# Chosen experts of a two-layer decoder: four places for the weighed rows, and weights laid out in pieces of 2 KB

## The chip, the cores and the metric

The kernel runs on one core of a Trainium2 chip. The metric is the device time of one execution in microseconds, the median of several runs. Before the change it is 2603.03 us (3 runs, 2599.43 to 2603.57).

## What is computed

The program is a two-layer decoder on 8 sequences of 512 tokens, width 256. Only its last part matters here, the mixture of experts of layer 1: 64 experts, each token goes to its 8 best, no more than 160 tokens an expert. Cut to that:

```python
def _swiglu(x, w1, w2):
    h = x @ w1.T
    x1, x2 = jnp.split(h, 2, axis=-1)
    return x1 * jax.nn.silu(x2) @ w2.T
# x: 4096 tokens x 256; expert_w1: 64 x 1536 x 256; expert_w2: 64 x 256 x 768
shared_out = _swiglu(x, shared_w1, shared_w2)
w_topk, idx_topk = jax.lax.top_k(softmax(x @ wg.T), 8)       # then w_topk / sum
buf = zeros((64, 160, 256)).at[expert, rank].set(x[token])   # gather by expert
h = jnp.einsum('ech,efh->ecf', buf, expert_w1)
x1, x2 = jnp.split(h, 2, axis=-1)
out = jnp.einsum('ecf,ehf->ech', x1 * jax.nn.silu(x2), expert_w2)
combined = zeros((4096, 256)).at[token].add(out * weight)
return shared_out + combined
```

## The kernel before

All arithmetic is float32. `mix_experts_sparse` is the last phase. Its first block computes the shared expert, the gates and, for each expert, the list of its tokens. It also writes normalised rows with their gates to `token_rows` in HBM, and the residual stream to `out_x` in HBM. SyncE loads the weights of experts 0 and 1 during this block.

Its second block is the part for the chosen experts; it takes the last 0.7 ms. Each engine walks over the 64 experts in the same order (`experts_in_turn`, L2077), four experts to a turn (`GATHERED`). An expert has 160 rows: 128 **main rows** (`xa`, `index_a`, `oa`) and 32 **tail rows**; the tails of four experts share one tile (`xb`, `index_b`, `ob`, 32 partitions, a "quad", for each).

- SyncE loads expert e's weights with two DMAs (`load_expert`, L2118 and L2119) as soon as expert e-2 has done its first products (the wait on `h_full` of `after_first_product`, L2515). `w1` has two places, `w2` four.
- TensorE, for each expert: 48 products of the first layer (L2616, six steps of eight, into three places of `hp`), then 12 of the second layer (L2623, into `op`), in whose middle it transposes the next expert's gathered rows (L2588, L2592). After an odd expert it does the second layer for the tails of the pair (`tails`, L2602).
- ScalarE applies silu (L2640). VectorE multiplies the halves (L2684) and so frees a place of `hp` (`h_free`); in between it weighs the main rows of the expert before (L2661: `op` times the gate, to `oa`, counted by `weighed`), and after each pair the tails (L2674, L2676, to `ob`).
- GpSimd adds the weighed rows to `out_x` by indirect DMAs with addition (`scatter`, L2529) and gathers the rows of expert e+4 (L2130, tails L2136). Two scatters may hit the same token, so a main scatter waits until all scatters of the experts before it have landed (semaphore `added`).

The places of `oa` are kept by the semaphore `rows_free`. GpSimd puts 2 in at the start (L2573), and one more each time an expert's turn comes in which all earlier main scatters have landed (L2549 for even places, L2553 for odd ones). VectorE waits at L2660 for `rows_free` to reach e+1 before it weighs expert e. Its queue is in order: while it waits there, the products of L2684 for the current expert wait behind it, no place of `hp` comes free, and TensorE's next step of L2616 waits. `tails_free` does the same for the single place of `ob` (L2554).

The weights lie in HBM as one array, a row for each expert and partition: 3072 numbers (12 KB) for `w1` and 1536 (6 KB) for `w2`. A DMA of L2118 so reads 128 pieces of 12 KB, one of L2119 128 pieces of 6 KB.

Of the kernel before, what the change touches and what calls it, by code (L numbers as in the profile page):

```python
# [16 lines left out]
P = 128  # L17
B, S, D = 8, 512, 256
NT = B * S // P
TB = S // P  # L20
DC = D // P
# [2048 lines left out]

GATHERED = 4


# [10 lines left out]
def mix_experts_sparse(nc, ctx, x, ident, stats, mean, rstd, w_gate, w_exp, sw_in, sw_out, rows, out):  # L2084


    with ExitStack() as own:
        k = Kit(nc, own, "me_")
# [27 lines left out]
        def load_expert(sp, e, place, w2_of):  # L2116
            one = w_exp[bass.ds(e, 1)].rearrange("a p n -> p (a n)")
            sp.dma_start(w1[:, place % 2].rearrange("p c n -> p (c n)"), one[:, 0:DC * 2 * F]).then_inc(w1_loaded[place % 2], 16)  # L2118
            sp.dma_start(w2_of.rearrange("p c n -> p (c n)"), one[:, DC * 2 * F:]).then_inc(w2_loaded[place], 16)  # L2119

# [372 lines left out]
        hid = k.sb("hid", [P, 2, FC, CAP])  # L2493
        oa = k.sb("oa", [P, 2, D])
        ob = k.sb("ob", [P, D])
# [15 lines left out]
        with nc.Block() as block:  # L2511
# [15 lines left out]
            def _(pool):  # L2527
# [8 lines left out]
                def turn(i, first, last):  # L2536
# [3 lines left out]
                    for m in range(GATHERED):  # L2540
# [5 lines left out]
                        if m % 2 == 0:  # L2546
                            all_added(i * (32 * GATHERED), 32 * m)
                            if not (first and m == 0):
                                pool.sem_inc(rows_free, 1)  # L2549
                            scatter(oa[:, m % 2, :], then_a[:, m % 2, :])  # L2550
                        else:
# [10 lines left out]
                            pool.sem_inc(passed, 1)  # L2562
                            scatter(oa[:, m % 2, :], then_a[:, m % 2, :])
                            scatter(ob[quad(m), :], then_b[:, 1, :])
# [7 lines left out]

                pool.sem_inc(rows_free, 2)  # L2573
                pool.sem_inc(tails_free, 1)
# [70 lines left out]
            def _(dve):  # L2645
# [11 lines left out]
                def weigh(e, place):  # L2657

                    dve.wait_ge(o_full, e + 1)
                    dve.wait_ge(rows_free, e + 1)  # L2660
                    nc.vector.tensor_scalar(oa[:, place % 2, :], op[:, place % 2, 0:D], xa[:, place, bass.ds(e + D, 1)], None, ALU.mult)\  # L2661
                        .then_inc(weighed, 1)
# [105 lines left out]
def laid_out(i):  # L2768
# [3 lines left out]
    def by_partition(w):  # L2772

        n, c, m = w.shape[0], w.shape[1] // P, w.shape[2]
        return w.reshape(n, c, P, m).transpose(0, 2, 1, 3).reshape(n, P, c * m)

    def slices(w, axis):
# [11 lines left out]
    a["L0_ffn_w_out"] = w2  # L2789
    a["L1_ffn_w_exp"] = np.concatenate([by_partition(i["L1_ffn_expert_w1"].transpose(0, 2, 1)),  # L2790
                                        by_partition(i["L1_ffn_expert_w2"].transpose(0, 2, 1))], axis=2)
    for name in ("L0_attn_out_w", "L1_xattn_Wo", "L1_ffn_wg",
# [20 lines left out]
```

## Time and profile before

| | |
|---|---|
| median of 3 runs | 2603.03 us |
| the profiled execution: time | 2608.1 us |
| the profiled execution: span | 2606.3 us |
| TensorE busy, whole span | 2210.4 us, 85% |
| VectorE | 1300.6 us, 50% |
| ScalarE | 821.2 us, 32% |
| GpSimd | 833.1 us, 32% |
| DMA traffic | 412.86 MB, mean 158 GB/s |
| first transposes of the chosen experts | at 1890.77 us of the span |

The profile is one execution. Shares over the whole span mix phases with different limits; the part for the chosen experts must be read by itself. In the views, PE is TensorE, PEld its weight loads, DVE VectorE, ACT ScalarE, POOL GpSimd, SP SyncE; an engine name with a q is that engine's queue of DMAs and semaphores. Times are microseconds from the start of the span, "mean ns" nanoseconds. "Idle before" an operation is followed by what released it.

### The profile page before, as it was taken

To read this page: it belongs to the slowest core of one execution; us is meant where nothing else is said; L and a number is where in the kernel's file an instruction comes from. 1 tells how busy PE (TensorE), PEld (TensorE's weight loads), DVE (VectorE), ACT (ScalarE), POOL (GpSimd) and SP (SyncE) were. 2 spreads that over 40 slices of the span, in tenths; PEclk is the share of its full clock that TensorE was granted. 3 is DMA by queue.
4 is the path that set the end of the run, shared out by engine and by line. 5 is a ranking of instruction groups with operands and counts; after the bars stand their busy time and mean duration, and the time that the engine had idled before them with its cause. 6 is when DMAs were issued, how large, how long until landed. Compare 5 with 4: busy or idle time off the path is not lost. (4 is left out here: it accounts for less than half of the span.)

```text
span 2606.3 us, 39064 instructions
## 1 busy us (share of the span) xinstructions
PE 2210.4 (85%) x11638; PEld 1487.9 (57%) x11639; DVE 1300.6 (50%) x2816; ACT 821.2 (32%) x1855; POOL 833.1 (32%) x1016
## 2 busy tenths in 40 slices
PE   6999759719999556888888887999999999999996
PEld 3445436507777322333343334656588888888885
DVE  5554246534444475776767673579133333333332
ACT  2222303204444224565555664311111111111111
POOL 2100016760000436444552110222324444444444
PEclk9999859859999778998999998999999999999998
DMA  9996117324555545433442112210067777777774
GB/s 323 372 369 221 45 43 271 116 102 146 156 158 156 150 100 114 93 69 87 102 111 81 48 34 84 106 32 16 29 213 253 253 252 252 250 248 248 250 253 134
DMA packets 254145, 412.86 MB, mean 158 GB/s; under 512 B 29960, under 2 KB 224113, under 8 KB 245852
## 3 DMA queue, kind: packets, MB, share of 16 engines
q1 hardware_dynamic: 215388, 351.92, 39.7%
q0 software_dynamic: 38656, 59.70, 10.5%
q8 instruction: 50, 0.82, 0.1%
q14 instruction: 51, 0.42, 0.1%
HBM read 262.05 MB, written 148.89 MB: 158 GB/s over the span
## 5 line engine op out<-in xcount | busy, mean ns | idle before, releaser
L2616 PE MATMUL me_hp<-me_xgT,me_w 128*128 128x160 f32 x3072 | 444.3, 303 | 27.0 <-DVE me_hid L2684 26.3
L2616 PEld LDWEIGHTS me_hp<-me_xgT,me_w 128*128 128x128 f32 x3072 | 421.7, 191 | 57.0 <-DVE me_hid L2684 33.5
L1371 DVE TENSOR_REDUCE hd_nmax<-hd_wide 128x2 f32<-128x1024 f32 x256 | 307.5, 1218 | 132.5 <-PE hd_wide L1116 131.8
L1300 ACT ACTIVATE hd_prob<-hd_slim 128x512 f32<-128x512 f32 x512 | 276.3, 602 | 193.5 <-PE hd_slim L1127 193.0
L2640 ACT ACTIVATE me_act_out<-me_hp 128x160 f32<-128x160 f32 x384 | 116.4, 303 | 591.2 <-PE me_hp L2616 545.4
L2684 DVE TENSOR_TENSOR me_hid<-me_act_out,me_hp 128x160 f32<-128x160 f32 x384 | 121.5, 320 | 316.9 <-ACT me_act_out L2640 311.4
L1127 PE MATMUL hd_slim<-hd_q_stack,hd_k_stack 100*128 100x512 bf16 x512 | 200.6, 395 | 43.8 <-ACT hd_prob L1300 31.9
L1116 PE MATMUL hd_wide<-hd_k_stack,hd_q_stack 97*128 97x512 bf16 x512 | 202.0, 399 | 30.6 <-DVE hd_rest L1365 15.8
L2529 POOL DMA_INDIRECT out_x<-me_oa,me_then_a x64 | 101.6, 1588 | 253.8 <-DMA out_x<-me_ob,me_then_b 241.0
L1999 PE MATMUL mr_e_hp<-mr_w,mr_e_xtT 128*128 x640 | 167.8, 385 | 0.8 <-issue 0.8
L2276 PE MATMUL me_r_hp<-me_r_xnT,me_r_sw 128*128 128x512 f32 x384 | 167.8, 593 | 0.0
L1127 PEld LDWEIGHTS hd_slim<-hd_q_stack,hd_k_stack 100*128 100x128 bf16 x512 | 50.3, 99 | 199.3 <-ACT hd_prob L1300 84.7
L999 POOL DMA_INDIRECT all_x<-outputs,rt_place x96 | 150.3, 1565 | 28.4 <-issue 28.4
L1687 POOL DMA_INDIRECT places<-mr_s_xg,mr_s_place x128 | 131.0, 1023 | 57.9 <-issue 38.7
L1139 PE MATMUL hd_pv<-hd_prob,hd_v 128*32 128x512 f32 x1024 | 138.1, 611 | 3.9 <-ACT hd_oT L1263 3.6
L2055 DVE TENSOR_TENSOR mr_e_hid<-mr_e_act_out,mr_e_hp 128x128 f32<-128x128 f32 x160 | 46.0, 287 | 190.7 <-ACT mr_e_act_out L2031 190.7
L2233 POOL TENSOR_TENSOR me_r_hid<-me_r_act_out,me_r_up_out 128x512 f32<-128x512 f32 x48 | 64.5, 1343 | 214.1 <-ACT me_r_up_out L2332 214.1
L1993 PE MATMUL mr_e_xp<-all_ident,mr_e_xt 128*128 128x128 f32 x320 | 63.2, 280 | 74.6 <-DMA mr_e_xt<-places 57.5
L2276 PEld LDWEIGHTS me_r_hp<-me_r_xnT,me_r_sw 128*128 128x128 f32 x384 | 72.5, 191 | 84.7 <-issue 84.3
L1999 PEld LDWEIGHTS mr_e_hp<-mr_w,mr_e_xtT 128*128 128x128 f32 x640 | 110.4, 193 | 10.2 <-issue 1.4
L2026 ACT ACTIVATE mr_e_xtT<-mr_e_xp 128x256 f32<-128x256 f32 x160 | 61.3, 383 | 134.6 <-PE mr_e_xp L1993 134.3
L1116 PEld LDWEIGHTS hd_wide<-hd_k_stack,hd_q_stack 97*128 97x128 bf16 x512 | 50.3, 100 | 87.2 <-DVE hd_nmax L1371 26.5
(385 smaller groups left out, 3679.4 us busy)
## 6 DMA issues: line engine op xcount, KB each, us to landing
me_w<-in_L_ffn_w_exp SPq DMA_DIRECT2D x64, 1536.0 KB, 6.9
places<-z_zero SPq DMA_DIRECT2D x64, 1152.0 KB, 11.4
me_w_first<-in_L_ffn_w_exp SPq DMA_DIRECT2D x32, 768.0 KB, 8.9
me_w_second<-in_L_ffn_w_exp SPq DMA_DIRECT2D x32, 768.0 KB, 9.0
mr_e_xt<-places SPq DMA_DIRECT2D x160, 144.0 KB, 2.1
outputs<-mr_e_y SPq DMA_DIRECT2D x160, 128.0 KB, 1.7
part_rows<-hd_parts SPq DMA_DIRECT2D x48, 256.0 KB, 2.4
hd_k_stack<-part_rows SPq DMA_DIRECT2D x192, 64.0 KB
```

The source lines that it names most:

```text
L999: nc.gpsimd.indirect_dma_start(out=x[:, r * TB + j, :], out_offset=None, in_=outputs[:, :], in_offset=bass.IndirectOffsetOnAxis(ap=place[: ...
L1116: last = nc.tensor.matmul(wide[:, at, j, :], q_stack[0:FIRST_ROWS, bt.slot, h, qc * P:(qc + 1) * P], k_stack[0:FIRST_ROWS, bt.slot, h, :], ...
L1127: nc.tensor.matmul(slim[:, slim_slot(bt, item), :], k_stack[:, bt.slot, h, kc * P:(kc + 1) * P], q_stack[:, bt.slot, h, :], start=True, st ...
L1139: last = nc.tensor.matmul(pv[32 * j:32 * j + 32, :], v[:, slot, kc, head(g, j), :], prob[:, kc * GH + j, :], start=(kc == 0), stop=(kc == ...
L1300: nc.scalar.activation(prob[:, u, :], slim[:, slim_slot(bt, item), :], ACT.Exp, scale=D ** -0.5)\
L1371: nc.vector.tensor_reduce(nmax[:, g % 2, n // 2, c:c + 2], wide[:, at], AX.X, ALU.max, negate=True)\
L1687: nc.gpsimd.indirect_dma_start(out=places[:, :], out_offset=bass.IndirectOffsetOnAxis(ap=place[:, b * TB + j, n:n + 1], axis=0), in_=xg[:, ...
L1999: last = nc.tensor.matmul(hp[:, v, 0:2 * F], xtT[:, v, c, :], w1[:, bass.ds(e, 1), c, :].rearrange("p a n -> p (a n)"), start=(c == 0), st ...
L2276: last = nc.tensor.matmul(hp[:, u % 2, half, :], sw1[:, c, at:at + P], xnT[:, c, b * S:(b + 1) * S], start=(c == 0), stop=(c == DC - 1))
L2616: last = nc.tensor.matmul(hp[:, f % 3, half * CAP:(half + 1) * CAP], w1[:, sl, c, cols], xgT[:, sl, c, :], start=(c == 0), stop=(c == DC - 1))
L2640: nc.scalar.activation(act_out[:, f % 2, :], hp[:, f % 3, CAP:2 * CAP], ACT.Silu).then_inc(silu_done, 1)
L2684: nc.vector.tensor_tensor(hid[:, sl, f, :], act_out[:, f % 2, :], hp[:, f % 3, 0:CAP], ALU.mult).then_inc(h_free, 1)
```

## The change

`oa` gets four places in place of two, one for each expert of a turn. GpSimd puts 4 into `rows_free` at the start, so that VectorE, to weigh expert e, waits for GpSimd to have come to expert e-3 where it was e-1. Scatters read the place of their expert.

The array of expert weights is laid out anew, on the host, as 64 experts x 9 pieces x 128 partitions x 512 numbers. Six pieces are `w1`, three are `w2`. The DMAs read 128 x 6 and 128 x 3 pieces of 2 KB. Their number, their bytes and their targets in SBUF are the same.

```diff
--- before.py
+++ after.py
@@ -2069,6 +2069,7 @@
 
 
 GATHERED = 4
+W_PIECE = 512
 
 
 def experts_in_turn(eng, n, one):
@@ -2114,9 +2115,12 @@
         index_ready, y_stored = s.sem("index_ready"), s.sem("y_stored")
 
         def load_expert(sp, e, place, w2_of):
-            one = w_exp[bass.ds(e, 1)].rearrange("a p n -> p (a n)")
-            sp.dma_start(w1[:, place % 2].rearrange("p c n -> p (c n)"), one[:, 0:DC * 2 * F]).then_inc(w1_loaded[place % 2], 16)
-            sp.dma_start(w2_of.rearrange("p c n -> p (c n)"), one[:, DC * 2 * F:]).then_inc(w2_loaded[place], 16)
+            one = w_exp[bass.ds(e, 1)].rearrange("a c p n -> p (a c) n")
+            n1 = DC * 2 * F // W_PIECE
+            sp.dma_start(w1[:, place % 2].rearrange("p c n -> p (c n)").rearrange("p (c n) -> p c n", c=n1), one[:, 0:n1, :])\
+                .then_inc(w1_loaded[place % 2], 16)
+            sp.dma_start(w2_of.rearrange("p c n -> p (c n)").rearrange("p (c n) -> p c n", n=W_PIECE), one[:, n1:, :])\
+                .then_inc(w2_loaded[place], 16)
 
         def take(pool, now, index, count):
 
@@ -2491,7 +2495,7 @@
         xgT = k.sb("xgT", [P, 2, DC, CAP])
         act_out = k.sb("act_out", [P, 2, CAP])
         hid = k.sb("hid", [P, 2, FC, CAP])
-        oa = k.sb("oa", [P, 2, D])
+        oa = k.sb("oa", [P, GATHERED, D])
         ob = k.sb("ob", [P, D])
         gates_b = k.sb("gates_b", [P, E])
         xp = k.ps("xp", [P, S])
@@ -2547,7 +2551,7 @@
                             all_added(i * (32 * GATHERED), 32 * m)
                             if not (first and m == 0):
                                 pool.sem_inc(rows_free, 1)
-                            scatter(oa[:, m % 2, :], then_a[:, m % 2, :])
+                            scatter(oa[:, m, :], then_a[:, m % 2, :])
                         else:
                             pool.wait_ge(added, i * (32 * GATHERED) + 32 * m - 16)
                             pool.sem_inc(rows_free, 1)
@@ -2560,7 +2564,7 @@
                             scatter(ob[quad(m - 1), :], then_b[:, 0, :])
                             pool.wait_ge(added, i * (32 * GATHERED) + 32 * m)
                             pool.sem_inc(passed, 1)
-                            scatter(oa[:, m % 2, :], then_a[:, m % 2, :])
+                            scatter(oa[:, m, :], then_a[:, m % 2, :])
                             scatter(ob[quad(m), :], then_b[:, 1, :])
                         if not last:
                             count = count + 1
@@ -2570,7 +2574,7 @@
                                 count = count + 1
                                 gather_tails(pool, i + 1, count)
 
-                pool.sem_inc(rows_free, 2)
+                pool.sem_inc(rows_free, GATHERED)
                 pool.sem_inc(tails_free, 1)
                 pool.wait_ge(y_stored, 16 * B)
                 turn(0, True, False)
@@ -2658,7 +2662,7 @@
 
                     dve.wait_ge(o_full, e + 1)
                     dve.wait_ge(rows_free, e + 1)
-                    nc.vector.tensor_scalar(oa[:, place % 2, :], op[:, place % 2, 0:D], xa[:, place, bass.ds(e + D, 1)], None, ALU.mult)\
+                    nc.vector.tensor_scalar(oa[:, place, :], op[:, place % 2, 0:D], xa[:, place, bass.ds(e + D, 1)], None, ALU.mult)\
                         .then_inc(weighed, 1)
 
                 def weigh_tails(e, pair, place, odd):
@@ -2787,8 +2791,9 @@
     a["L0_xattn_bq"] = np.tile(i["L0_xattn_bq"], B).reshape(P, 1)
     a["L0_ffn_w_in"] = by_partition(np.concatenate([w1, w3], axis=2))
     a["L0_ffn_w_out"] = w2
-    a["L1_ffn_w_exp"] = np.concatenate([by_partition(i["L1_ffn_expert_w1"].transpose(0, 2, 1)),
-                                        by_partition(i["L1_ffn_expert_w2"].transpose(0, 2, 1))], axis=2)
+    w_exp = np.concatenate([by_partition(i["L1_ffn_expert_w1"].transpose(0, 2, 1)),
+                            by_partition(i["L1_ffn_expert_w2"].transpose(0, 2, 1))], axis=2)
+    a["L1_ffn_w_exp"] = np.stack(np.split(w_exp, w_exp.shape[2] // W_PIECE, axis=2), axis=1)
     for name in ("L0_attn_out_w", "L1_xattn_Wo", "L1_ffn_wg",
                  "L1_ffn_shared_w1", "L1_ffn_shared_w2"):
         a[name + "T"] = i[name].T
```

No instruction changes its place on any engine. The one thing that differs in the order of instructions, beside line numbers, is the shape of SyncE's loads of weights. SyncE, in its loop over turns of four experts, the loads of the first and the second expert of a turn (the `ISA` rows are waits and addresses):

```order
-L2118 DMA me_w<-in_L_ffn_w_exp 128x3072
-L2119 ISA
-L2119 DMA me_w_first<-in_L_ffn_w_exp 128x1536
-L2515 ISA
-L2118 ISA
-L2118 DMA me_w<-in_L_ffn_w_exp 128x3072
```

and with the change:

```order
+L2120 DMA me_w<-in_L_ffn_w_exp 128x6x512
+L2122 ISA
+L2122 DMA me_w_first<-in_L_ffn_w_exp 128x3x512
+L2519 ISA
+L2120 ISA
+L2120 DMA me_w<-in_L_ffn_w_exp 128x6x512
```

Each DMA stays at its place behind the same wait; only its pieces are other.

## Rows read from the trace of the kernel before

**Rows 1.** Busy time by engine (PE, PEld, DVE, ACT, POOL), granted clock, DMA share, GB/s.
```profile
1940.00:2560.00 620.00, 594.83 (x4235) 530.20 (x4234) 219.05 (x646) 103.61 (x342) 275.75 (x371) 1.00 0.74 250
```

**Rows 2.** The chain that ended last, shares of the whole span by line.
```profile
DMA out_x<-me_ob,me_then_b 14%; POOL out_x L2529 2%; POOL me_xa L2130 1%; PE me_hp L2616 1%; POOL me_then_b L2123 0%; DMA out_x<-me_oa,me_then_a 0%; POOL me_now_a L2123 0%; POOL me_then_a L2123 0%; PE me_op L2623 0%; POOLq L2123 0%; POOLq L2124 0%; POOL me_now_b L2123 0%; POOLq L2125 0%; POOLq L2511 0%; PE me_tp L2602 0%
```

**Rows 3.** Who waited for whom, 1900 to 2550 us: total, times, longest.
```profile
POOL out_x L2529 <- DMA out_x<-me_ob,me_then_b: 228.9, 56, 7.4
DVE me_oa L2661 <- POOLq L2549: 72.6, 28, 4.0
```

**Rows 4.** GpSimd in order of time: start, us, operation, idle before it.
```profile
2301.69 1.57 POOL L2529 DMA_INDIRECT out_x<-me_oa,me_then_a  x1 [5.82 <-DMA out_x<-me_ob,me_then_b]
2303.57 1.32 POOL L2529 DMA_INDIRECT out_x<-me_ob,me_then_b  x1 [0.30 <-issue]
...
2310.61 1.60 POOL L2529 DMA_INDIRECT out_x<-me_oa,me_then_a  x1 [3.43 <-DMA out_x<-me_ob,me_then_b]
...
2318.57 1.38 POOL L2529 DMA_INDIRECT out_x<-me_ob,me_then_b  x1 [1.01 <-issue]
2322.69 1.59 POOL L2529 DMA_INDIRECT out_x<-me_oa,me_then_a  x1 [2.73 <-DMA out_x<-me_ob,me_then_b]
...
2332.17 1.60 POOL L2529 DMA_INDIRECT out_x<-me_oa,me_then_a  x1 [3.97 <-DMA out_x<-me_ob,me_then_b]
...
2338.04 1.36 POOL L2529 DMA_INDIRECT out_x<-me_ob,me_then_b  x1 [0.97 <-POOL me_then_b L2123]
```

**Rows 5.** TensorE at the start of the part: the first-layer products of experts 1 to 4.
```profile
1903.29 6.78 PE L2616 MATMUL me_hp<-me_xgT,me_w 128*128 128x160 f32 x48
...
1914.25 6.79 PE L2616 MATMUL me_hp<-me_xgT,me_w 128*128 128x160 f32 x48
...
1923.70 6.78 PE L2616 MATMUL me_hp<-me_xgT,me_w 128*128 128x160 f32 x48
...
1934.88 5.70 PE L2616 MATMUL me_hp<-me_xgT,me_w 128*128 128x160 f32 x40
```

**Rows 6.** TensorE: an even expert in the steady part, and the last expert.
```profile
2303.95 5.70 PE L2616 MATMUL me_hp<-me_xgT,me_w 128*128 128x160 f32 x40
2310.82 1.35 PE L2616 MATMUL me_hp<-me_xgT,me_w 128*128 128x160 f32 x8 [1.17 <-DVE me_hid L2684]
...
2576.96 6.73 PE L2616 MATMUL me_hp<-me_xgT,me_w 128*128 128x160 f32 x48
...
2586.21 1.50 PE L2602 MATMUL me_tp<-me_w_second,me_hid 128*32 128x256 f32 x24
```

**Rows 7.** DMA queues, 1900 to 2550 us: packets, MB, share of 16 engines.
```profile
q1 hardware_dynamic: 17280, 141.57, 58.1%
q0 software_dynamic: 14632, 21.48, 16.0%
```

**Rows 8.** All DMA traffic, 388 to 412 us: loads of an earlier layer's expert weights.
```profile
DMA packets 5444, 8.87 MB, mean 370 GB/s; under 512 B 139, under 2 KB 2331, under 8 KB 5443
```

**Rows 9.** SyncE: a load of 768 pieces, one of 128, and the landing of `me_w`.
```profile
L2200 SPq DMA_DIRECT2D me_r_sw<-in_L_ffn_shared_w2T x1: 462/462/462, 1598.2 to 1598.2; - x1
...
2312.34 0.34 SPq L2118 DMA_DIRECT2D me_w<-in_L_ffn_w_exp  x1
...
DMA to landing us min/median/max: 6.4/6.9/9.0
```

**Rows 10.** The end of the program: GpSimd's scatters, then VectorE's last operation.
```profile
2583.68 1.32 POOL L2529 DMA_INDIRECT out_x<-me_ob,me_then_b  x1 [0.30 <-issue]
...
2588.66 1.57 POOL L2529 DMA_INDIRECT out_x<-me_oa,me_then_a  x1 [3.45 <-DVE me_oa L2661]
...
2594.14 1.34 POOL L2529 DMA_INDIRECT out_x<-me_ob,me_then_b  x1 [0.91 <-POOL me_then_b L2123]
2597.80 1.55 POOL L2529 DMA_INDIRECT out_x<-me_oa,me_then_a  x1 [2.32 <-DMA out_x<-me_ob,me_then_b]
...
2589.55 0.99 DVE L2676 SCALAR_TENSOR_TENSOR me_ob<-me_tp,me_gates_b,me_ob 32x256 f32<-32x256 f32 x2
```

## The prediction

> **What bounds the kernel now.** I read the stretches first: the change touches only the part for the chosen experts, about 1890 us to the end. There [rows 1] TensorE is busy 594.83 of 620 us at full granted clock and the DMA engines 74%. So some 4% of idle time is on offer, and the question is who makes it. The chain of waits [rows 2] gives TensorE's first products 1% and the weights nothing: 14% of the whole span, half of the 27% that this part takes, is the landing of one kind of transfer, the scatter of tail rows `out_x<-me_ob` on GpSimd's queue. The table of waits [rows 3] agrees: GpSimd waits 228.9 us for that scatter, in 56 pieces, and VectorE waits 72.6 us, in 28 pieces, for GpSimd's count `rows_free` (the wait of L2660, released at L2549), that is for a free place of `oa`. GpSimd waits for VectorE only at the start and the end. So GpSimd and its scatters are a loop that never rests, and it sets the pace.
>
> The pace, by pairs of experts. GpSimd's timeline [rows 4] shows one pair: scatter of the odd main rows at 2301.69, of its tails at 2303.57; the next main scatter must wait for both to land and goes at 2310.61, 7.04 us later; then a gather, the indices and the tails' gather until 2318.57; then again a landing, 4.12 us, to 2322.69. The three DMA-free pieces are 1.88 and 7.96 us (5.87 in the other pair of a turn, 2332.17 to 2338.04, where no tails are gathered), so 8.8 us a pair on average. TensorE's timeline without a stall [rows 5]: first products start at 1903.29, 1914.25, 1923.70 and 1934.88, so 10.96 and 11.18 us after an odd expert (the tails' products, and in one of two the transposes of gathered tails) and 9.45 after an even one. In the steady part [rows 6] the even expert that starts at 2303.95 stands still for 1.17 us before its last eight first-layer products, because VectorE stood in the wait for `rows_free`.
>
> **The loss in total.** Expert 1 starts at 1903.29 [rows 5], expert 63 at 2576.96 [rows 6]: 673.67 us for 31 pairs, 21.73 each. Without stalls the same steps are 31 x 9.45 + 16 x 10.96 + 15 x 11.18 = 636.0 us, 20.5 a pair. TensorE loses 37.7 us, 1.2 us a pair.
>
> **Part 1: weights in pieces.** The DMAs of L2118 and L2119 stay as many and as large; their pieces go from 12 KB and 6 KB to 2 KB, so 72 packets per DMA engine and expert in place of 16 (9 x 128 / 16 and 2 x 128 / 16). What it costs: queue 1 (the weights) took 58.1% of 16 engines over 650 us for 141.57 MB [rows 7], 0.52 us per 12 KB. The nearest row for 2 KB pieces from HBM is the load of the first experts' weights, earlier in this kernel: 5444 packets, 8.87 MB, of 2 KB and less, at 370 GB/s [rows 8], so 0.07 us a packet or 0.09 us for 2 KB. 72 x 0.09 = 6.4 us an expert, as now (16 packets of mean 9 KB, 6.3 us). Cost nothing; the cover is that first-layer weights, issued at 2312.34, land after 6.9 us, 9.0 at most [rows 9], and are needed when the next expert of that parity starts, at 2326.02: 13.7 us. It is lost only with transfers twice as slow. Issuing: a DMA with 768 pieces took SP 462 ns and one with 128 took 340 ns [rows 9], so at most 0.3 us more per expert on SP, inside the same cover. The first two experts are loaded ahead, under the shared expert, long before use.
>
> What it frees: a scatter of 128 rows puts 8 packets on each engine and the tails' 2 more, behind the first. If each waits for one packet of weights, ten of them cost 5.2 us now and 0.9 us with 2 KB. The row to hold against this is the end of the kernel, where no weights move [rows 10]: from the tail scatter at 2583.68 to the main scatter that waited for it at 2588.66 are 4.98 us, against 7.04 under load, and the lone tail scatter's stretch is 3.66 (2594.14 to 2597.80) against 4.12. Mean under load is 21.73 - 8.8 = 12.9 us of landings a pair; without load 8.6. So the surplus is 4.3 us a pair, and the effect of smaller pieces lies between 0 and 4.3. I take 3.6 (5.2 less 0.9 is 83% of 5.2, and 83% of 4.3 is 3.6), nearer to the unloaded end, since the weights' share of an engine stays and only the grain changes. GpSimd's loop then takes 18.1 us a pair, below TensorE's 20.5. It is enough if 1.2 of the 4.3 us go, 28%.
>
> A rule of the Trainium skill bears on this. The page "DMA: Bandwidth & Descriptors", section on queues, rings and completion order, says that an engine turns between queue rows packet by packet, and that a typical packet holds 9 to 17 descriptors; by the first half the scatters are relieved as I take it, by the second several 2 KB pieces would make one turn and the sum would be nothing at all. That is rival B.
>
> **Part 2: four places for `oa`.** No instruction is added: the same operations of L2661, one an expert, write to four places, and GpSimd frees four at the start. VectorE's weighing of expert e now needs GpSimd to have come to e-3, not e-1. Alone this is worth nothing in the steady part: a loop that never rests keeps its 21.7 us, TensorE gains a lead of two experts and then waits as before, and the end is set by the last scatter. With part 1 it is the cushion for single late landings (the longest wait was 7.4 us in all, and VectorE's longest 4.0). At nothing, covered by part 1.
>
> What is late next: `tails_free`. GpSimd gives it after it saw the odd expert's weighing, one copy later; in the stretch without stalls VectorE did not wait there, so nothing is charged.
>
> **The end.** TensorE ends at 2587.7 [rows 6] and the last tail scatter but one goes only at 2594.14, 6.4 us later, since GpSimd is behind. With GpSimd in front it follows VectorE's two steps of 0.99 us [rows 10] and some 0.3 us, so 2.3 us after TensorE: 4.1 us less.
>
> **Sum**: 37.7 + 4.1 = 41.8 us off. The profiled execution took 2608.1 us (span 2606.3), 5.1 above the median of 2603.03; from the median, 2561 us.
>
> **Rivals.**
> A, partial relief (12%): the landings hang on HBM or on bytes more than on the grain, the loop falls to between 20.5 and 21.6 us a pair. For it: the unloaded rows carry no gather beside the scatter either, so part of the surplus is the gather's. Against it: 28% suffices. Half the needed relief gives 31 x 0.6 = 19 us and half of the end, about 2582; the case spans 2570 to 2597.
> B, the change doesn't do what it says (10%): pieces are still served in long runs, the loop keeps 21.73, four places only shift the lead: 2603, within 2 us.
> C, slower (8%): a packet has a fixed price and the weights become the bound. The rows for it are those of GpSimd's queue: 14632 packets in 16.0% of 16 engines over 650 us [rows 7] are 0.114 us each, for 1.5 KB. If 2 KB pieces cost in proportion, 0.159 us, then 72 x 0.159 + 1.7 (GpSimd's packets per expert) = 13.2 us per expert against 10.87 now, 62 x 2.3 = 143 us more: about 2746. It decides from (10.87 - 1.7) / 72 = 0.127 us a packet. Against it stands [rows 8] with 0.09, for the same direction and size.
>
> **Chances.** Forecast 70%: 2555 to 2569, from a tail or a cushion that gives a little more or less, and the spread of the runs (4 us). What a measurement can tell from no change is about 0.2%, 5 us. Faster holds the forecast and A, 82%; same is B, 10%; slower is C, 8%. The range for 8 in 10 is the forecast and most of A: 2554 to 2592.
>
> **What the next profile would show.** Right: in the chain of waits TensorE's first products take the place of `out_x<-me_ob`; GpSimd waits for VectorE's weighing; the wait at the weighing is gone and first products start 9.45 us after an even expert; the stretches of 7.04 and 4.12 us become about 5 and 3.7; the first-layer weights still land in some 7 us; each expert's 256 packets of weights are 1152. Wrong: landings of scatters as before with TensorE idle 4% (B), weights landing after 10 us or more and TensorE waiting for them (C), or a new wait of VectorE for `tails_free`.

## The result, and the profile after

The change made the kernel slower: 2625.08 us (4 runs, 2623.22 to 2627.07) against 2602.55 us, a ratio of 1.0084 with a 95% interval of 1.0068 to 1.0100. The forecast was 2561 us, with a range from 2554 to 2592. The profiled execution has a span of 2624.5 us against 2606.3.

The stretch of [rows 1] in the changed kernel (columns as there):

```profile
1940.00:2560.00 620.00, 578.32 (x4074) 520.91 (x4073) 210.50 (x614) 99.45 (x329) 264.55 (x358) 0.96 0.76 242
```

TensorE is busy 578 us where it was busy 595, and its granted clock has fallen from 1.00 to 0.96. The chain that ended last, as in [rows 2]:

```profile
DMA out_x<-me_ob,me_then_b 12%; DMA out_x<-me_oa,me_then_a 4%; POOL out_x L2533 2%; PE me_hp L2620 1%; POOL me_xa L2134 1%; POOL me_then_b L2127 0%; PE me_op L2627 0%; POOL me_now_a L2127 0%; POOLq L2127 0%; POOL me_then_a L2127 0%; POOLq L2128 0%; POOLq L2129 0%; POOLq L2515 0%; POOL me_now_b L2127 0%; PE me_tp L2606 0%
```

The tail scatters still lead the chain, with 12% where they had 14%, and 4% of the main scatters `me_oa`, which had 0%, come on top. The loop of GpSimd still sets the pace. Who waited for whom, as in [rows 3], 1920 to 2570 us:

```profile
POOL out_x L2533 <- DMA out_x<-me_ob,me_then_b: 212.9, 50, 6.3
...
PE me_xp L2592 <- DMA me_xa<-token_rows,me_now_a: 41.6, 7, 6.1
POOL me_then_b L2127 <- DMA out_x<-me_oa,me_then_a: 40.3, 15, 4.3
```

VectorE's wait for a place of `oa` is gone, as forecast. In its place TensorE waits for gathered rows, seven times, 6 us each, and GpSimd waits 40.3 us for the landing of main scatters before it may send the tails. The same wait in the kernel before (1900 to 2550 us):

```profile
POOL me_then_b L2123 <- DMA out_x<-me_oa,me_then_a: 3.6, 8, 0.5
```

TensorE's timeline shows one of the seven stops:

```profile
1993.81 6.79 PE L2620 MATMUL me_hp<-me_xgT,me_w 128*128 128x160 f32 x48
2000.43 1.89 PE L2627 MATMUL me_op<-me_w_second,me_hid 128*128 128x256 f32 x8
2008.17 0.69 PE L2592 MATMUL me_xp<-all_ident,me_xa 128*128 128x128 f32 x2 [5.85 <-DMA me_xa<-token_rows,me_now_a]
2008.65 1.91 PE L2627 MATMUL me_op<-me_w_second,me_hid 128*128 128x256 f32 x4
```

TensorE stands for 5.85 us in the middle of the second layer, before the next expert's transposes; GpSimd gathers an expert's rows only after it has sent the scatter of the expert four before, and TensorE has run up to that. The four products after the stop take 1.91 us where four take 1.03 us in the same place of an expert without a stop. The stretch behind the stop shows why (columns as in [rows 1]):

```profile
2008.20:2010.40 2.20, 2.20 (x7) 1.84 (x8) 0.56 (x2) 0.00 (x0) 1.19 (x2) 0.50 0.94 272
```

The granted clock is 0.50 there, the lower of its two levels (1.2 GHz, not 2.4).

The queues and the landing of the weights, as in [rows 7, 9], 1900 to 2550 us (for `me_w`: number, KB of one, median us to landing):

```profile
q1 hardware_dynamic: 69505, 138.52, 61.3%
q0 software_dynamic: 14111, 20.66, 15.6%
...
me_w<-in_L_ffn_w_exp SPq DMA_DIRECT2D x58, 1536.0 KB, 7.8
```

The packets are smaller as told, they take 61.3% of the engines for 138.52 MB where it was 58.1% for 141.57, so 8% more for each byte, and the first-layer weights land after 7.8 us, not 6.9.

**Where the time is.** From the first main scatter to the last tail scatter, GpSimd's timeline has 691.5 us before (1908.12 to 2599.66) and 712.7 after (1905.33 to 2618.03): 21.2 us more, which covers the loss (18.2 us between the two profiled spans, 22.5 between the medians). Worked out from each kernel's timeline of GpSimd, the mean of 31 pairs of experts, in us; "M" is a main scatter, "T" one of tails, and the piece from the odd M to its T is 1.88 in all of them. The kernels e1 to e14 are explained below:

| kernel | even M to T | T to odd M | T to next even M | pair | ratio to before |
|---|---|---|---|---|---|
| before | 7.08 | 5.69 | 7.31 | 21.95 | 1 |
| the change | 8.16 | 5.96 | 6.65 | 22.64 | 1.0084 |
| e1, pieces of 2 KB only | 7.09 | 6.34 | 6.83 | 22.13 | 1.0036 [1.0009, 1.0063] |
| e2, four places only | 8.38 | 5.74 | 7.22 | 23.22 | 1.0134 [1.0087, 1.0181] |
| e3, no loads | 10.43 | 3.74 | 4.55 | 20.60 | one run |
| e4, four places, tails at once | 6.87 | 4.83 | 7.18 | 20.75 | 0.9886 [0.9839, 0.9934] |
| e5, the change again | 8.15 | 5.98 | 6.62 | 22.62 | 1.0074 [1.0045, 1.0102] |
| e6, four places, two free | 7.08 | 5.91 | 7.09 | 21.95 | 1.0001 [0.9977, 1.0026] |
| e7, four places, three free | 8.72 | 5.96 | 6.51 | 23.06 | 1.0148 [1.0116, 1.0181] |
| e8, pieces of 1 KB only | 7.10 | 6.21 | 6.63 | 21.82 | one run |
| e9, the change, tails at once | 6.89 | 5.20 | 6.84 | 20.80 | 0.9853 [0.9829, 0.9877] |
| e10, two places, tails at once | 7.20 | 6.21 | 7.98 | 23.26 | 1.0141 [1.0114, 1.0168] |
| e11, loads one step later | 8.42 | 6.31 | 6.36 | 22.96 | 1.0112 [1.0087, 1.0137] |
| e12, loads two steps later | 8.56 | 7.15 | 5.07 | 22.67 | 1.0096 [1.0067, 1.0124] |
| e13, first-layer loads only | 7.09 | 4.38 | 7.44 | 20.78 | one run |
| e14, loads apart | 8.79 | 5.55 | 5.91 | 22.13 | one run |

The change's loss of 0.7 us a pair stands in the first column: from the even main scatter to the tails it takes 1.1 us more, while the two stretches in which GpSimd waits for tail scatters (the second and third columns) take 12.6 us together where they took 13.0. The first piece holds a wait too: before GpSimd sends the tails, it waits for the even main scatter to land.

The runs were made on more than one chip, and the kernel before took from 2602 to 2660 us on them, by other parts of the program (e6, with a ratio of 1.0001, has the same 691.5 us from first to last scatter); so times are compared as ratios within a group, and the times that the first expectations name are those of the first chip.

### The profile page after: what moved, and what is told of

Same layout as the page of the kernel before. It is cut to its first block and busy times, and to the rows that moved or that the text cites. A ratio compares the mean times of both kernels' runs of the same rounds, so it can differ in the third digit from the quotient of the medians.

```text
span 2624.5 us, 39064 instructions
## 1 busy us (share of the span) xinstructions
PE 2211.6 (84%) x11638; PEld 1496.8 (57%) x11639; DVE 1303.9 (50%) x2816; ACT 821.2 (31%) x1855; POOL 832.9 (32%) x1016
## 5 line engine op out<-in xcount | busy, mean ns | idle before, releaser
L2620 PEld LDWEIGHTS me_hp<-me_xgT,me_w 128*128 128x128 f32 x3072 | 430.4, 194 | 23.1 <-issue 20.4
L2280 PEld LDWEIGHTS me_r_hp<-me_r_xnT,me_r_sw 128*128 128x128 f32 x384 | 72.3, 190 | 84.5 <-issue 84.1
L2026 ACT ACTIVATE mr_e_xtT<-mr_e_xp 128x256 f32<-128x256 f32 x160 | 61.3, 383 | 134.5 <-PE mr_e_xp L1993 134.2
```

The lines of the kernel that those rows point to most:

```text
L2280: last = nc.tensor.matmul(hp[:, u % 2, half, :], sw1[:, c, at:at + P], xnT[:, c, b * S:(b + 1) * S], start=(c == 0), stop=(c == DC - 1))
L2620: last = nc.tensor.matmul(hp[:, f % 3, half * CAP:(half + 1) * CAP], w1[:, sl, c, cols], xgT[:, sl, c, :], start=(c == 0), stop=(c == DC - 1))
```

## Experiments: each half alone, and no loads at all

**e1** keeps the new layout and goes back to two places (the second main scatter and VectorE's weighing likewise).

```diff
-        oa = k.sb("oa", [P, GATHERED, D])
+        oa = k.sb("oa", [P, 2, D])
-                            scatter(oa[:, m, :], then_a[:, m % 2, :])
+                            scatter(oa[:, m % 2, :], then_a[:, m % 2, :])
-                pool.sem_inc(rows_free, GATHERED)
+                pool.sem_inc(rows_free, 2)
```

> The change's layout in pieces of 2 KB, with two places of oa as before. Theory 'pieces': small packets of weights take more turns at the DMA engines and stretch the landings of scatters and gathers; then nearly all of the loss is here, about 2620 us, and the wait of VectorE for a free place is longer than 2.6 us a pair. Theory 'places': the loss comes from TensorE running ahead with four places; then this kernel stands at 2603 us within 5. The theory of my prediction (2 KB pieces relieve the scatters) would give 2565 to 2580 us here, since two places suffice once landings are short.

It took 2666.64 us against 2655.97. The forecast's idea falls. Five scatters of GpSimd's timeline in this kernel,

```profile
2168.76 1.60 POOL L2533 DMA_INDIRECT out_x<-me_oa,me_then_a  x1 [2.56 <-DMA out_x<-me_ob,me_then_b]
...
2174.64 1.36 POOL L2533 DMA_INDIRECT out_x<-me_ob,me_then_b  x1 [0.97 <-POOL me_then_b L2127]
2181.08 1.57 POOL L2533 DMA_INDIRECT out_x<-me_oa,me_then_a  x1 [5.08 <-DMA out_x<-me_ob,me_then_b]
2182.95 1.32 POOL L2533 DMA_INDIRECT out_x<-me_ob,me_then_b  x1 [0.30 <-issue]
...
2189.81 1.60 POOL L2533 DMA_INDIRECT out_x<-me_oa,me_then_a  x1 [3.25 <-DMA out_x<-me_ob,me_then_b]
```

show 6.44 us from the lone tail scatter at 2174.64 to the next main one, and 6.86 from the one at 2182.95: in the mean these two stretches are 6.34 and 6.83 us, where the kernel before has 5.69 and 7.31. One grew, the other shrank, and together they are as long as with packets of 12 KB (13.17 us, not 13.00). The pieces cost 0.1 to 0.6% by themselves.

**e2** makes the other half of the change alone: four places in the old layout.

> Four places of oa, weights in pieces of 12 KB and 6 KB as before. Theory 'places': TensorE runs up to four experts ahead, is stopped by the gather of rows instead, for some 6 us at a time, the loads of weights lose their fixed place between the scatters, and GpSimd's pair of experts takes 22.4 us or more in place of 21.7: about 2620 to 2630 us. Theory 'pieces': GpSimd's pair stays at 21.7 us and the time at 2603 us within 5.

It took 2692.65 us, a ratio of 1.0134 where the whole change has 1.0084. Pairs now take from 17.8 to 27.4 us, where before nearly all took 21.2 to 22.0. One of the worst, on GpSimd, and SyncE's load beside it:

```profile
2388.77 1.60 POOL L2529 DMA_INDIRECT out_x<-me_oa,me_then_a  x1 [4.08 <-DMA out_x<-me_ob,me_then_b]
...
2398.19 0.17 POOL L2123 COPY me_then_b<-me_tails 32x1 int32 x1 [3.49 <-DMA out_x<-me_oa,me_then_a]
...
2399.78 1.38 POOL L2529 DMA_INDIRECT out_x<-me_ob,me_then_b  x1 [1.01 <-issue]
...
2389.37 0.34 SPq L2118 DMA_DIRECT2D me_w<-in_L_ffn_w_exp  x1
```

The load goes out at 2389.37, 0.6 us after the main scatter. That scatter lands only at about 2398, and the tails go 11.0 us after it. The nine pairs in which a load goes out from 0.6 us before to 0.9 us after the even main scatter have 10.2 to 11.3 us in this piece, all others but the first and the last 5.9 to 8.6. So "places" is the part that costs. The two more places cost 1.3%, the pieces 0.4%; together they cost 0.8% in the change and 0.7% in **e5**, its repeat, less than the sum. No run separates why smaller pieces soften the other half; what the traces say of it stands below, under "what holds a scatter".

> The changed kernel as it is, once more, beside the other parts. By the first runs, pieces alone gave 1.004 of before and places alone 1.013. If the two effects add, this gives about 1.017; if the smaller pieces soften what the places cost, as the shorter pair of the changed kernel (22.6 us against 23.2 us with places alone) says, it lies between: 1.006 to 1.011.

**e3** takes the loads out of the loop of the changed kernel, and TensorE's waits for them (the experts then compute with weights of earlier ones, so this is no version to use). The main lines of the edit:

```diff
-                with sp.Fori(1, TURNS_OF_4) as i:
-                    for m in range(GATHERED):
-                        after_first_product(i * GATHERED + m, m)
-                    pe.wait_ge(w1_loaded[sl], t * 32 + 16 * (place // 2) + 16)
+                    pe.wait_ge(w1_loaded[sl], 16)
```

> The changed kernel without the loads of first-layer weights from expert 2 on and of second-layer weights from expert 4 on, and without TensorE's waits for them: the experts compute with weights of earlier experts; all else moves as before. If the weights' traffic is what holds scatters and gathers, the tail scatter lands in about 3 us in place of 6, the gather in 3 in place of 6, GpSimd's pair takes under 18 us, TensorE becomes the bound at 20.5 us a pair and the time is about 2560 to 2568 us. If landings are set by the scatters themselves or by GpSimd's own queue, they stay at 5 to 6 us and the time at 2600 or more.

On its chip it took 2614.59 us in one run against 2655.97, 41 us less. GpSimd's timeline and TensorE's busy time:

```profile
2051.26 1.38 POOL L2532 DMA_INDIRECT out_x<-me_ob,me_then_b  x1 [2.36 <-DVE me_ob L2679]
2055.02 1.57 POOL L2532 DMA_INDIRECT out_x<-me_oa,me_then_a  x1 [2.37 <-DMA out_x<-me_ob,me_then_b]
2056.89 1.33 POOL L2532 DMA_INDIRECT out_x<-me_ob,me_then_b  x1 [0.30 <-issue]
...
2061.47 1.60 POOL L2532 DMA_INDIRECT out_x<-me_oa,me_then_a  x1 [0.97 <-POOL me_then_a L2127]
...
1990.00:2560.00 570.00, 570.00 (x4141) 515.12 (x4141) 211.99 (x620) 100.97 (x332) 270.56 (x361) 1.00 0.23 36
```

The tail scatter's stretch is 3.76 us alone and 4.58 behind a main one, TensorE is busy for all of 570 us, and the pair takes 20.6 us. The 4.58 us are no landing any more: that scatter's idle time is ended by GpSimd's own copy of the indices. So the floor that the prediction worked out for TensorE (20.5) was right, the unloaded stretches (3.66 and 4.98) nearly so, and it was right that the weights' traffic holds the landings. What failed is the way by which the landings were to get shorter, and what was taken to stay as it is.

## Experiments: is it the lead, the memory, or where the loads fall?

In the kernel before, GpSimd's `rows_free` releases VectorE's weighing, which releases TensorE's last step, after which SyncE sends the next load. That ties the loads to the scatters. SyncE's timeline there:

```profile
2321.81 0.33 SPq L2118 DMA_DIRECT2D me_w<-in_L_ffn_w_exp  x1
...
2333.92 0.33 SPq L2118 DMA_DIRECT2D me_w<-in_L_ffn_w_exp  x1
```

The main scatters of [rows 4] go at 2310.61 and 2332.17; loads follow at 2312.34 [rows 9], 2321.81 and 2333.92, that is 1.7 and 11.2 us behind, and in 28 of the 29 pairs between the first and the last they follow at 1.7 to 1.8 and 11.1 to 11.4 us. With four places nothing ties them, and TensorE, quicker than the loop, moves its loads past the scatters until it is stopped, and begins again. In the changed kernel one pair met the load at a bad point:

```profile
2341.73 1.60 POOL L2533 DMA_INDIRECT out_x<-me_oa,me_then_a  x1 [3.76 <-DMA out_x<-me_ob,me_then_b]
...
2349.75 0.17 POOL L2127 COPY me_then_b<-me_tails 32x1 int32 x1 [4.16 <-DMA out_x<-me_oa,me_then_a]
...
2351.30 1.36 POOL L2533 DMA_INDIRECT out_x<-me_ob,me_then_b  x1 [0.97 <-POOL me_then_b L2127]
...
2341.51 0.37 SPq L2120 DMA_DIRECT2D me_w<-in_L_ffn_w_exp  x1
```

The load at 2341.51 is 0.2 us ahead of the main scatter; the tails' indices wait for its landing until 2349.75, and the tails go 9.57 us after it, where [rows 4] has 5.87 for the pair of a turn in which, as here, no tails are gathered.

**e6** and **e7** have four places in the old layout, with two and with three free at the start. For e6, against the change:

```diff
-                pool.sem_inc(rows_free, GATHERED)
+                pool.sem_inc(rows_free, 2)
```

> Four places of oa in the old layout of weights, but GpSimd frees only two at the start, so that VectorE may be no further ahead than before the change. Theory 'running ahead': the place in memory costs nothing, the lead does; time within 0.3% of before and VectorE's wait for a free place back, TensorE's 6 us waits for gathered rows gone. If the tile itself mattered (other addresses, more memory), the time stays at 1.01 or more.

> As the last, with three places free at the start: a lead of one expert more than before. Theory 'running ahead': TensorE is still stopped by the count of places, once a pair, so the loads of weights keep a fixed place against the scatters, but another one than before; the pair of experts is regular, and its length tells whether the old place was a lucky one: 21.0 to 23.5 us, never scattered between 18 and 27 as with four free. If only the loss of a fixed place costs, the time is within 0.5% of before; if the old place was the good one, 1.005 to 1.015.

e6 took 2660.18 us against 2659.55. Its waits, 2000 to 2600 us:

```profile
POOL out_x L2529 <- DMA out_x<-me_ob,me_then_b: 216.3, 54, 5.8
DVE me_oa L2661 <- POOLq L2549: 72.3, 28, 3.6
```

VectorE's wait for a place is back, 72.3 us in 28, and with it the time and the pair of 21.95. The memory costs nothing; the lead (how far VectorE and TensorE may be ahead of GpSimd) does. e7 took 2697.48 us against 2659.55, in the range that was given, but my picture of it was wrong: its pairs are not regular (17.8 to 26.0 us), and TensorE is stopped by the gather there too. One expert of lead is enough to untie the loads.

**e11** and **e12** test the place of the loads without any lead: two places, old layout, and SyncE sends each load one or two steps later.

```diff
-                    sp.wait_ge(h_full, e * FC - FC)
+                    sp.wait_ge(h_full, e * FC - FC + 1)
```

> The kernel before, but SyncE issues an expert's weights one step of six later (after the first eight products of the next expert), so the loads come some 2.9 and 12.4 us after the even main scatter in place of 1.7 and 11.2; two places, so the place of the loads stays fixed. TensorE's cover for the loads (13.7 us for a landing of 7) is far from gone. Theory 'where the loads fall against the scatters sets the loop': in the kernel with four places alone, pairs with loads at 2.5 to 3.7 us took 22.2 to 23.5 us, against 21.7 in the kernel before, so 15 to 45 us slower, ratio 1.006 to 1.017, with the same lead and the same memory as before. Rival 'the lead itself costs, by TensorE's 6 us stops and what follows them': no change, ratio within 0.3% of 1.

> As the last with two steps, some 4 and 13.5 us after the even main scatter: the lone tail scatter (sent 6 to 8 us after the main one) then meets more of the first load, the pair of scatters sent at 12 us goes ahead of the second. Theory 'where the loads fall': another length than with one step, between 21.0 and 23.5 us a pair, regular from pair to pair. Rival: within 0.3% of before.

2637.85 and 2630.47 us against 2605.51: 1.011 and 1.010 with the same memory, the same lead and the same bytes. With one step the pairs wander from 17.1 to 30.3 us, and the place of the loads with them, which I had not expected. With two the pairs are mostly 22.0 to 22.8 us, as in this one, with SyncE's loads below it:

```profile
2135.50 1.60 POOL L2529 DMA_INDIRECT out_x<-me_oa,me_then_a  x1 [0.97 <-POOL me_then_a L2123]
...
2143.77 1.38 POOL L2529 DMA_INDIRECT out_x<-me_ob,me_then_b  x1 [1.01 <-issue]
2151.09 1.59 POOL L2529 DMA_INDIRECT out_x<-me_oa,me_then_a  x1 [5.95 <-DMA out_x<-me_ob,me_then_b]
2152.99 1.34 POOL L2529 DMA_INDIRECT out_x<-me_ob,me_then_b  x1 [0.30 <-issue]
...
2157.57 1.60 POOL L2529 DMA_INDIRECT out_x<-me_oa,me_then_a  x1 [0.97 <-POOL me_then_a L2123]
...
2132.60 0.33 SPq L2118 DMA_DIRECT2D me_w<-in_L_ffn_w_exp  x1
...
2143.63 0.34 SPq L2118 DMA_DIRECT2D me_w<-in_L_ffn_w_exp  x1
```

The loads fall 2.9 us ahead of the even main scatter and 8.1 behind it (the expectation had 4 and 13.5 behind it). The lone tail scatter at 2143.77, just beside a load, has a stretch of 7.32 us; but the next stretch is only 4.58 us, as with no loads, and the two together are shorter than before the change, 12.2 us in the mean where they were 13.0. What grew is the piece from the even main scatter to the tails, 8.56 us where it was 7.08, with GpSimd's wait for this scatter to land.

The landing of the even main scatter, found one by one in the traces of 29 pairs (the first and the last left out), says why. In the kernel before, the load goes out 1.7 to 2.2 us behind it in every pair, and it lands after 3.7 to 4.0 us, as it does at the end of the kernel with no load at all (3.8). GpSimd's own work up to the tails' indices takes about as long, so the landing is hardly waited for. In [rows 4], before the tails that go at 2338.04:

```profile
2336.50 0.17 POOL L2123 COPY me_then_b<-me_tails 32x1 int32 x1 [0.46 <-DMA out_x<-me_oa,me_then_a]
```

With a load 2.6 to 3.2 us ahead of it (23 pairs of e12) it lands after 6.2 to 7.0 us, with one 1.0 to 1.3 us behind it (five pairs of e11) after 8.6 to 9.7. So what counts is not that the place of the loads is fixed but which it is. The kernel before had a good one, because a load 1.7 us behind the even main scatter leaves its landing as it is with no load; the scatters of the odd expert had a load beside them before the change too. In every kernel of the table that is slower by its loads (the change, e2, e5, e7, e11, e12, e14) the first piece has grown to 8.2 to 8.8 us, and in none of them are the two other stretches together longer than before.

## Experiments: what holds a scatter

For scatters sent between 2000 and 2500 us, each one's landing (found one by one in the trace) is 5.66 us in the mean of 91 before and 5.38 in the mean of 89 after. Those over 70% of whose flight lies in a load of weights take 6.26 us (68 of them) and 6.08 (66); ten in the changed kernel with under 30% take 2.91, nine of them tails. In the mean the size of the pieces hardly shows; the load does. At the same place against a load it does show, in both directions. An even main scatter whose load goes out within 0.2 us of it lands after 8.8 and 9.0 us with packets of 12 KB (one in e11, one in e12) and after 7.6 to 8.2 with 2 KB (four in the changed kernel, eight in e9); with the load 1.2 to 1.4 us behind, three take 8.6 to 8.9 us with 12 KB (e11), and two 4.7 with 2 KB (the change and e9). Against that a load in packets of 2 KB lasts longer (7.8 us, not 6.9), and an odd main scatter sent some 2 us after it goes out takes 7.4 us in the mean of 19 (the change and e9), where it takes 6.6 in the mean of eight with 12 KB (the kernel before and e11). This fits with two stretches that change in opposite ways in e1, and with a softer loss from four places; these are few scatters, and no run tests it alone.

Three kernels ask what it is about the load.

**e8** has pieces of 1 KB (`W_PIECE = 256`) and two places.

> Two places, weights in pieces of 1 KB. If what a scatter waits for is a run of several packets of weights, it halves again against pieces of 2 KB, and the two landings of a pair (13.2 us together with 2 KB, 13.0 with the old pieces) fall to 12 or less. If it waits for the weights' bytes, they stay at 13 us or grow with the weights' own landing, which the page of the profile would show at 8 us or more; time then 2 to 20 us above that of pieces of 2 KB.

One run took 2655.57 us, inside the spread of the kernel before (2644.78 to 2666.14, median 2659.55) and not above the ratio of the 2 KB pieces as I had expected, and the two stretches together 12.84 us, against 13.17 with 2 KB and 13.00 with 12: under a tenth of what the loads cost (13.0 less 8.3), if anything.

**e13** leaves the second-layer loads out of the kernel before (its experts too compute with weights of others), **e14** sends them four steps after the first-layer ones.

> The kernel before without the loads of second-layer weights from expert 4 on (the experts compute their second layer with those of experts 0 to 3): the loads of an expert are over some 2 us earlier. If a scatter's landing is held by a load in progress, whatever its pieces, the two landings of a pair (13.0 us before, 8.3 us with no loads) fall by about a third of the difference, to some 11.4 us, the pair comes near TensorE's 20.5 us and the time is 20 to 40 us under before. If it is held by the number of DMAs or of packets in front of it, not by their bytes, the landings stay above 12.5 us: half of the packets of weights are gone, but a scatter meets as many first-layer packets as before.

> The kernel before, with the second-layer weights issued four steps of six (some 4.4 us) after the first-layer ones: same bytes, same pieces, but no long queue of 2.3 MB at a time. If a scatter waits for the backlog that stands in front of it when it is sent, both landings shorten somewhat (sum 12 us or less) and the pair is under 21.5 us. If it waits as long as any load is in progress, spreading the loads lengthens the time in which one is, and the pair takes 22 us or more: ratio 1.005 to 1.015.

Both have one run. e13 took 2575.01 us against 2601.64. The stretches are 4.38 and 7.44 us, 11.8 together, nearer to the 11.4 of the first case than to 12.5, and GpSimd still waits for landings in them, never for VectorE (1990 to 2540 us); TensorE has no stall, and the pair takes 20.8 us. A third less load is enough to make TensorE the bound. e14 took 2618.69 us, 1.007. Both stretches shortened (5.55 and 5.91), but the piece behind the even main scatter grew to 8.79: in 15 of 29 pairs a second-layer load goes out from 0.7 us before to 0.3 us after that scatter, and it lands after 7.0 to 9.7 us; the pairs go from 18.3 to 27.7 us. Neither case comes out clean: what is taken from one scatter is given to another. What is shown is that a load in progress holds the scatters, and that cutting its packets, down to a twelfth of their size, gains nothing over a whole pair. By which rule the DMA engines share stays open.

## A version that beats both

The new wait of the changed kernel is GpSimd's, for the landing of the even main scatter ahead of the same expert's tails. They are other tokens, so nothing needs it but the count of free places. Against the change:

```diff
-                            pool.wait_ge(added, i * (32 * GATHERED) + 32 * m - 16)
-                            pool.sem_inc(rows_free, 1)
                             pool.sem_inc(tails_free, 1)
...
                             pool.wait_ge(added, i * (32 * GATHERED) + 32 * m)
-                            pool.sem_inc(passed, 1)
+                            pool.sem_inc(rows_free, 1)
                             scatter(oa[:, m, :], then_a[:, m % 2, :])
```

**e4** has this with four places and the old layout.

> Four places of oa, old pieces, and GpSimd no longer waits at an odd expert for the main scatter of the even expert before it sends that same expert's tails (their rows are distinct tokens); the free place is handed out one wait later. If that landing is what made GpSimd's loop longer when TensorE runs ahead (8.2 us from main scatter to tails in the changed kernel, 7.1 before), the piece falls to 6.9 us at most, the pair to about 21 us, and the time to 2580 to 2595 us. If the tails' own landing takes up what is saved (it waits behind the main rows in the same queue), the pair stays at 22 us and the time within 10 of the kernel with four places alone.

2623.22 us against 2655.97, 0.9886, somewhat better than the first case said. GpSimd's timeline, and TensorE's busy time:

```profile
2123.19 1.60 POOL L2529 DMA_INDIRECT out_x<-me_oa,me_then_a  x1 [4.18 <-DMA out_x<-me_ob,me_then_b]
...
2131.00 1.38 POOL L2529 DMA_INDIRECT out_x<-me_ob,me_then_b  x1 [1.01 <-issue]
2134.81 1.57 POOL L2529 DMA_INDIRECT out_x<-me_oa,me_then_a  x1 [2.44 <-DMA out_x<-me_ob,me_then_b]
2136.68 1.32 POOL L2529 DMA_INDIRECT out_x<-me_ob,me_then_b  x1 [0.30 <-issue]
...
2143.76 1.60 POOL L2529 DMA_INDIRECT out_x<-me_oa,me_then_a  x1 [3.47 <-DMA out_x<-me_ob,me_then_b]
...
1960.00:2580.00 620.00, 619.88 (x4487) 559.18 (x4486) 232.42 (x677) 109.14 (x360) 287.75 (x387) 1.00 0.78 264
```

The two stretches of landings still take 3.81 and 7.08 us here, and the main scatter still meets a load sent 0.7 us after it (SyncE's timeline), but its landing is no longer waited for by itself: it passes beside 7.81 us of GpSimd's own work and the tails. In e9, which has each landing in its trace, 27 of 29 even main scatters land after 7.2 to 8.4 us, and TensorE does not stop all the same. In e4 it is busy 619.88 of 620 us at full clock.

**e10** has the same with two places.

> The kernel before with tails sent at once and two places: says whether the four places are needed for that gain. The second free place of a pair is now handed out only when the lone tail scatter has landed, 10 to 12 us after the even main scatter, and VectorE wants it at about 9.4: so a new wait of 1 to 3 us in the even weighing. If four places are needed, the time is 0.994 to 1.003 of before; if GpSimd's shorter loop is all that counts, 0.986 to 0.992 as with four.

It took 2646.81 us against 2605.51, 1.0141, slower than either case said: free places now come one landing later, and VectorE waits for them longer than the 72.6 us of [rows 3] (1950 to 2570 us),

```profile
DVE me_oa L2659 <- POOLq L2560: 93.8, 27, 6.0
```

so here the four places are needed. **e9** is the change as it stands, with tails at once:

> Four places, tails sent at once, and pieces of 2 KB: the change with one wait of GpSimd taken away. With old pieces that gave 0.989 of before, with TensorE the bound at 20.5 us a pair and no stall. TensorE stays the bound here, so the pieces show nothing: 0.986 to 0.992. If smaller pieces still cost through the loads' own landing (7.8 us in place of 6.9) it would be over 0.993.

2570.27 us against 2605.51, ratio 0.9853 (0.9829 to 0.9877), the best of all, 35 us under before. Its busy time, 1930 to 2550 us:

```profile
1930.00:2550.00 620.00, 619.96 (x4493) 559.76 (x4493) 232.47 (x678) 110.10 (x362) 288.63 (x386) 1.00 0.82 263
```

TensorE never rests. Whether the pieces help here was not told apart: e4 and e9 ran on other chips, and their intervals overlap.

## Why the prediction was wrong

- **What bounds the kernel**: right. GpSimd's loop through the landings of its scatters; e3, e4, e9 and e13, each of which shortens it in another way, all bring TensorE's stalls to nothing.
- **The loss in total**: right. TensorE's 20.5 us a pair, 37.7 us in all and 4.1 at the end: e3 gained 41 us and e9 35, each against the kernel before on its own chip.
- **"I take 3.6" of the surplus of 4.3 us**: this is the step that failed first, and with it the gain is gone. It took the landing under load as ten packets of the scatter that each wait for one packet of weights. In e1 the two stretches got longer, by 0.2 us a pair (13.17 against 13.00); in e8, in one run, shorter by 0.2. The row that I held against it, the unloaded end [rows 10], showed that the load matters and nothing about its grain. The lower end of my bound, 0, was the true one. I also misread that row: the scatter at 2588.66 was released by VectorE's weighing, so its 4.98 us are more than a landing; e3 has 4.58. The second half of what the Trainium skill's page "DMA: Bandwidth & Descriptors" says in its section on queues (a packet of many descriptors to a turn) speaks for this outcome, and rival B carried it with 10%; pieces of 1 KB changing little agrees with it, without proving it.
- **"A loop that never rests keeps its 21.7 us"**: this step failed too, and the sign hangs on it. The sum held the pieces between the landings fixed as "DMA-free" (7.96 and 5.87 us), though in them GpSimd waits for the even main scatter to land. How long it flies depends on where the loads fall; the loads are sent by TensorE's progress, and that was held in place by the very wait that the change takes away. This piece went from 7.08 us to 8.16 in the change and 8.38 in e2, and the pair from 21.95 to 22.64 and 23.22. I had named a cushion where the change removed a tie.
- **"Cost nothing" of part 1**: off by a little. The first-layer loads land after 7.8 us, not 6.9, and e1 is 0.4% slower. Rival C's price of packets did not come: 61.3% of the engines, no wait for weights.
- **The rivals**: none was this one. B, with 10%, had the landings right (unchanged together), and the loop unchanged too, at 2603 us. C was the only slower one, and by another cause, the weights as the bound at 2746 us.

## What to carry to other kernels

A wait that costs an engine a little can hold something else in step. Before you give a producer more room, look who else is paced by it, above all whose DMAs, and compare their issue times against the transfers on the critical loop; if they have the same offset in every turn, a wait may be doing that, and taking it away can cost what it seemed to give. More room pays only when the loop it feeds is no longer the bound: here the same four places cost 1.3% alone and, with one needless wait for a landing gone, gave 1.1%, and with the smaller pieces as well 1.5% (intervals that overlap).

## What the runs showed of the hardware

- Indirect scatters with addition, main and tail together, land after 6.26 us beside a load of weights in packets of 12 and 6 KB, and 6.08 us beside one in packets of 2 KB; at the end of the kernel before, with no load, a main one takes 3.8 and a tail one 2.9 us. With packets of 1 KB the loop through them hardly changed.
- A load sent within some 1.3 us after a scatter of 128 rows still holds it in packets of 12 KB: 8.6 to 9.7 us to landing in e11, some 9 in e2. With the load 1.7 us behind, as in the kernel before, it lands after 3.7 to 4.0 us, as with none.
- After stops of some 6 us TensorE's granted clock fell to 0.50 for a while, and over the part it was 0.96; with stops of about 1 us, once a pair, it was 1.00 [rows 1]. GpSimd's loop did not wait for it: but for the start and the end it waited for VectorE 0.8 us in all (the changed kernel, 1950 to 2550 us).
